# Windowed attention on 32x32 parts of TensorE: four head pairs apart, whole stages in a row, and queries written into their tiles by ScalarE

## The reference

```
q = Wq @ layernorm(x) + bq;  k = Wk @ ctx + bk;  v = Wv @ ctx + bv     # 128 x 1024 each
k, v padded by 8 and 7 columns; window(t) = columns t .. t+15
attn[h,t,:] = softmax(q[h,:,t] . k[h,:,window(t)] * 16**-0.5)
x = x + Wo @ (sum over the window of attn * v) + bo
z = layernorm(x);  w = the two largest gates of softmax(z @ gate_w.T), scaled to sum 1
x = x + sum_e w[:,e] * (z @ lora_A[e].T @ lora_B[e].T)                 # rank 64, 8 experts
```

## Time and profile before

| | |
|---|---|
| median of 3 runs | 1298.94 us |
| the profiled execution | 1300.73 us, its span 1298.8 us, so 1.9 us lie outside the span |
| PE / PEld busy | 94% / 82% of the span |
| DVE, ACT, POOL busy | 69%, 29%, 32% |
| granted TensorE clock, mean | 0.995 of full |
| largest groups on the chain that ended last | L318 (fp32r products), L350 (scores), L363 (weighted sums) |

### The profile page before, as it was taken

How to read it: one execution, slowest core, us unless ns; L and a number is a source line. 1 busy time by engine, 2 the same in 40 slices (tenths; PEclk the granted TensorE clock), 3 DMA queues, 4 the chain that set the end, 5 groups by cost and what they waited for, 6 DMA issues and landing times.

```text
span 1298.8 us, 34642 instructions
## 1 busy us (share of the span) xinstructions
PE 1225.5 (94%) x13953; PEld 1064.8 (82%) x14080; DVE 891.5 (69%) x2021; ACT 380.5 (29%) x553; POOL 416.1 (32%) x300
## 2 busy tenths in 40 slices
PE   3889999999999999999999999999999999999986
PEld 2778888888888888888888888888888888888875
DVE  3777667766767766767766767776767766767653
ACT  3332232322232322232322232322232322232211
POOL 3443333323333332332323333322332322333110
PEclk9989999999999999999999999999999999999999
DMA  6443433343443343443343443243443343443210
GB/s 214 79 88 67 99 91 75 83 90 62 97 91 81 77 97 64 88 93 75 81 95 60 95 92 88 70 99 67 83 93 87 70 99 64 85 93 76 58 40 33
DMA packets 427427, 108.44 MB, mean 83 GB/s; under 512 B 410001, under 2 KB 410129, under 8 KB 427153
## 3 DMA queue, kind: packets, MB, share of 16 engines
q1 hardware_dynamic: 427280, 106.13, 37.6%
HBM read 55.22 MB, written 16.78 MB: 55 GB/s over the span
## 4 chain that ended last, share of the span: by engine, by line
PE 91%; issue 3%; DVE 1%; DMA 1%; POOL 1%; SPq 1%; ACT 0%; POOLq 0%; DVEq 0%
PE bank_a L318 30%; PE bank_b L350 22%; PE bank_b L363 19%; PE bank_c L318 16%; PE bank_a L373 4%; DMA v_diag<-v_t 1%; POOL src_split L873 0%; SPq L237 0%; SPq L246 0%; POOL v_diag L878 0%; DMA ident<-ident_in 0%; DMA raw<-ctx 0%; DVE mid_split L767 0%; DMA q_diag<-q_xn 0%; POOL src_split L883 0%
## 5 line engine op out<-in xcount | busy, mean ns | idle before, releaser
L350 PE MATMUL bank_b<-k_sb,q_diag 64*64 64x32 f32 x8192 | 312.5, 222 | 31.2 <-issue 30.9
L350 PEld LDWEIGHTS bank_b<-k_sb,q_diag 64*64 64x64 f32 x8192 | 271.0, 136 | 83.9 <-issue 71.7
L363 PEld LDWEIGHTS bank_b<-prob_t,v_diag 128*128 128x128 f32 x2304 | 315.7, 192 | 23.8 <-DMA v_diag<-v_t 4.9
L363 PE MATMUL bank_b<-prob_t,v_diag 128*128 128x96 f32 (+2 forms) x2304 | 326.9, 270 | 4.6 <-DMA v_diag<-v_t 4.6
L318 PE MATMUL bank_a<-down_split,mid_split 128*128 128x264 f32 (+1 forms) x1536 | 267.5, 298 | 2.7 <-DVE mid_split L767 2.7
L867 POOL TENSOR_TENSOR prob<-prob,row_inv 128x512 f32<-128x512 f32 x128 | 146.4, 1144 | 323.4 <-DVE row_inv L726 323.4
L318 PE MATMUL bank_c<-src_split,w_split 128*128 128x512 f32 x576 | 221.1, 459 | 18.0 <-POOL src_split L873 14.2
L318 PEld LDWEIGHTS bank_a<-down_split,mid_split 128*128 128x128 f32 x1536 | 214.9, 189 | 15.9 <-ACT mid_split L548 3.0
L318 PE MATMUL bank_a<-up_split,ht_split 128*128 128x512 f32 x768 | 216.3, 405 | 4.0 <-DVE ht_split L808 3.6
L318 PEld LDWEIGHTS bank_a<-up_split,ht_split 128*128 128x128 f32 x768 | 138.2, 189 | 33.8 <-ACT ht_split L585 4.2
L733 DVE STREAM_TRANSPOSE prob_t<-prob 128x768 f32<-128x768 f32 x128 | 124.6, 973 | 30.4 <-POOL prob L867 30.4
(11 more groups left out here) (68 smaller groups left out, 1087.1 us busy)
## 6 DMA issues: line engine op xcount, KB each, us to landing
v_diag<-v_t SPq DMA_DIRECT2D x128, 132.0 KB, 3.8
raw<-x SPq DMA_DIRECT2D x32, 512.0 KB, 5.9
raw<-ctx SPq DMA_DIRECT2D x32, 512.0 KB, 3.4
q_diag<-q_xn SPq DMA_DIRECT2D x512, 32.0 KB, 2.4
resid_pair<-x SPq DMA_DIRECT2D x32, 512.0 KB, 3.4
out<-resid_pair SPq DMA_DIRECT2D x32, 512.0 KB, 2.6
v_diag<-up_w SPq DMA_DIRECT2D x1, 2048.0 KB, 9.3
prob_t<-down_w SPq DMA_DIRECT2D x1, 780.0 KB, 4.8
```

The costliest lines, as they stand in the source:

```text
L350: last = nc.tensor.matmul(bank_b[m % 2][rows, t * KT:(t + 1) * KT], q_diag[rows, m // 2, n, :], k_sb[rows, at:at + KT], start=False, stop= ...
L363: last = nc.tensor.matmul(bank_b[2 + m % 2][:, lo * PW:hi * PW], v_diag[:, n * P:(n + 1) * P], prob_t[:, at:at + (hi - lo) * KT], start=i ...
```

## The change

The attention is cut into 4 pairs of heads instead of 2 halves (scores) and one whole (weighted sums). `scores_chunk` issues for each tile 4 matmuls, on rows and columns 0-31, 32-63, 64-95 and 96-127 of the array, with a 32 x 32 stationary operand. `weighted_chunk` does the same for the weighted sums. Each of the 4 chunks of a stage is issued whole (`attend`: 64 matmuls of scores of `cur`, then 64 of weighted sums of `prev` or `cur`), without projection or expert matmuls in between, and those are issued as whole stages too.

- ScalarE writes `q_diag` straight from PSUM, with two activations of 128 x 1024 whose scale is a per-channel mask times 0.25 (even heads, odd heads), so the zeros of the blocks are written too. `place_q`, `q_placed` and the zeroing of `q_diag` are gone.
- `v_even` is v transposed in blocks by DVE, as before. The tiles with an odd number need v shifted by 16 keys, `v_odd`, which 8 DMAs of 16 rows x 4 KB copy from `v_even`. The zeroing of `v_diag` is gone.
- `prob` and `prob_t` lose their zero columns. `weights_transpose` is 128 x 512 instead of 128 x 768.
- `k_sb`, `attn`, `q_diag` and the v tiles get two buffers each, and the attention's split values get a tile of their own (`attn_split`).
- The order on ACT, DVE and POOL is rearranged to the new stages.

```diff
-            def scores_group(m, s):
-                for t, n in tiles(m, s):
-                    at = (m * CT + t) * QT
-                    for z in range(HALVES):
-                        rows = slice(z * HALF_P, (z + 1) * HALF_P)
+            def scores_chunk(cur, m):
+                keys = k_sb[cur.parity]
+                for t in range(CT):
+                    n = m * CT + t
+                    for g in range(PAIRS):
+                        rows = slice(PW * g, PW * (g + 1))
                         last = nc.tensor.matmul(bank_b[m % 2][rows, t * KT:(t + 1) * KT],
-                                                q_diag[rows, m // 2, n, :],
-                                                k_sb[rows, at:at + KT], start=False,
+                                                q_diag[rows, cur.parity, n, :],
+                                                keys[rows, n * QT:n * QT + KT], start=False,
                                                 stop=t == CT - 1, skip_group_check=True)
-            def weighted_group(m, s):
-                for i in ((0, 1, 2), (3, 4), (5, 6), (7, 8))[s]:
-                    lo, hi = max(2 * i - 1, 0), min(2 * i + 2, CT)
-                    at = m * PC + 2 * i * STRIDE - (2 * i - lo) * KT
-                    n = m * CT // 2 + i
-                    last = nc.tensor.matmul(bank_b[2 + m % 2][:, lo * PW:hi * PW],
-                                            v_diag[:, n * P:(n + 1) * P],
-                                            prob_t[:, at:at + (hi - lo) * KT],
-                                            start=i == 0, stop=i == CT // 2, skip_group_check=True)
+            def weighted_chunk(b, m):
+                for t in range(CT):
+                    n = m * CT + t
+                    values = (v_even, v_odd)[n % 2][b.parity][:, n // 2 * PW:(n // 2 + 1) * PW]
+                    at = n * PW
+                    for g in range(PAIRS):
+                        rows = slice(PW * g, PW * (g + 1))
+                        last = nc.tensor.matmul(bank_b[2 + m % 2][rows, t * PW:(t + 1) * PW],
+                                                values[rows], prob_t[rows, at:at + PW],
+                                                start=t == 0, stop=t == CT - 1, skip_group_check=True)
+                def attend(m, weighted, k):
+                    if weighted:
+                        open_weighted(weighted, k)
+                    if cur:
+                        if m == 0:
+                            pe.wait_ge(q_out, cur.count(2, 2))
+                        open_scores(cur, m)
+                        scores_chunk(cur, m)
+                    if weighted:
+                        weighted_chunk(weighted, k)
...
-                    nc.scalar.activation(q_xn2[:], bank_c[:], ACT.Identity, bias=bq_scaled[:], scale=SCALE).then_inc(q_out, 1)
+                    for h in range(2):
+                        nc.scalar.activation(q_diag[:, ahead.parity, :, h * QT:(h + 1) * QT],
+                                             bank_c[:].rearrange("p (n i) -> p n i", i=QT), ACT.Identity,
+                                             bias=bq_scaled[:, h:h + 1],
+                                             scale=consts[:, 4 + h:5 + h]).then_inc(q_out, 1)
...
+            def place_v(cur):
+                half = PW // 2
+                source, odd = v_even[cur.parity], v_odd[cur.parity]
                 for g in range(PAIRS):
-                    rows = slice(PW * g, PW * (g + 1))
-                    sp.dma_start(blocks[rows, :, PW * g:PW * (g + 1)],
-                                 v_t[rows, :].rearrange("p (n c) -> p n c", c=PW)).then_inc(v_placed, 16)
+                    low = slice(PW * g, PW * g + half)
+                    high = slice(PW * g + half, PW * (g + 1))
+                    sp.dma_start(odd[low, :], source[high, 0:T]).then_inc(v_placed, 16)
+                    sp.dma_start(odd[high, :], source[low, KT:KT + T]).then_inc(v_placed, 16)
```

More of the change, by code:

```diff
@@ L330, in project_pass @@
                                 source, half, True, True)
-            def tiles(m, s):
-                return [(t, m % 2 * CT + t) for t in range(s * CT // GROUPS, (s + 1) * CT // GROUPS)]
             def open_scores(cur, m):
@@ new lines, in step @@
+                attend(2, cur, 0)
+                if prev:
+                    pe.wait_ge(attn_hi, prev.count(1, 1))
+                    pe.wait_ge(attn_lo, prev.count(1, 1))
+                    if ahead:
+                        pe.wait_ge(q_out, ahead.count(2, 2))
+                    elif cur:
+                        pe.wait_ge(v_out, cur.count(1, 1))
+                    for n in range(6):
+                        last = project_pass(n, bank_c, 3, attn_split)
+                        if n % 3 == 2:
+                            last.then_inc(o_done, 1)
@@ new lines, in step @@
+                if old:
+                    for f in range(FK):
+                        down(1, f)
+                attend(3, cur, 1)
+                if old:
+                    pe.wait_ge(h_done, old.count(2, 2))
+                    transposes(bank_a, h_sb, range(EK)).then_inc(ht_done, 1)
+                if ahead:
+                    pe.wait_ge(ctx_hi, ahead.count(1, 1))
+                    pe.wait_ge(ctx_lo, ahead.count(1, 1))
+                    if prev:
+                        pe.wait_ge(x1_done, prev.count(2, 2))
+                    else:
+                        pe.wait_ge(q_out, ahead.count(2, 2))
+                    for n in range(6):
+                        last = project_pass(n, bank_c, 1, src_split)
+                    last.then_inc(k_done, 1)
@@ L503, in _ @@
+                if old:
+                    pe.wait_ge(ht_hi, old.count(1, 1))
+                    pe.wait_ge(ht_lo, old.count(1, 1))
+                    for n in range(2):
+                        for e in range(EK):
+                            up(n, e)
             steps(pe, step)
@@ L828, in step @@
                     layernorm_stats(1, x1, ln2_step, prev)
[L829 to L832 removed]
+                if cur:
+                    weights_sum(cur, 2)
+                if old:
+                    weigh_experts(old, 1)
                 if prev:
```

361 lines of the change are left out of this document (117 added, 244 removed).

## The result

The changed kernel takes 1613.2 us (median of 4 runs, 1599.7 to 1622.9), the kernel before 1298.8 us beside it: a ratio of 1.241, with a 95% interval of 1.231 to 1.252. It is slower by a quarter, where 1160 us was forecast. The profiled execution is one of 1606.4 us.

The account below looks back on a forecast made before the run. PE was taken as the bound (94% busy, step 39.1 us); a new step of 34.8 us, bound by the round from DVE to PE, takes 32 x (39.1 - 34.8) = 138 us off 1300.73: 1160 us, range 1095 to 1290.

Parts of the forecast that it names:

- The array's overlap: Attention matmuls on PE: four 32 x 32 parts work at once, a record's average near 7 ns.
- t: Time in ns per attention matmul on PE, 512 a step; forecast 14.5, a step being 21.3 + 0.512 t us.
- six-record cut: Timeline of six old score records ending at 0.36 us, read as pairs starting some 10 ns apart, one pair in 58 ns.
- PE's base, 21.3 us: PE's step without attention: 22.1 us, less 1.3 for fewer changes between matmul kinds, plus 0.5 for those that stay.
- The round through DVE: PE waits for DVE: 3.3 us ahead of `h_sb`'s transposes, 1.5 us ahead of the last product; step 34.8 us.
- q by ScalarE, the v copies: ACT's second q write, some 1.1 us more, is hidden; v tile lands at 11.9 us, wanted at 11.8, no cost.
- Half the overlap: Rival: only two parts work at once, t near 29, PE step 36.1 us, 1203 us; 0.26 together with late instructions.
- late instructions: Rival: PE's instruction blocks take 1.07 us, singly 1.9 us, t up to 29 ns; 1200 to 1290, shared chance 0.26.
- the number to keep: Break-even for attention on PE: at t = 35 ns the step equals 39.1 us; below it the change gains.
- The sum of 1160: Whole kernel: 32 steps x (39.1 - 34.8) = 138 us off 1300.73, giving 1163, about 1161, forecast 1160 us.
- The slower rival: Each attention record costs a fixed 29 ns, t = 58, PE step 51.0 us, 1680 us in all; chance 0.24.
- The 1550 us: If record starts average no less than 25 ns, 1024 records give 46.9 us a step, about 1550 us.

Follow-up runs that it names:

- e_pace: TensorE alone, without the attention kernel: long runs of small matmuls between runs of 32 large ones; 216.12 us (one run).
- e_whole2: Kernel before with attention in whole stages, `h_sb` transposes ahead of the k projection, output projection and last expert products behind the last weighted sums; 1218.2 us, ratio 0.937.
- after: The changed kernel itself, with attention on four 32 x 32 parts in whole stages; 1613.2 us, ratio 1.241 to the kernel before.
- e_mixed: Changed kernel, same matmuls in another PE order: half stages of 32 attention matmuls alternate with half projections and expert halves; 1474.9 us, ratio 1.136.
- e_pairs: Changed kernel with half the attention matmuls, each covering two neighbouring tiles with one tile's stationary operand; 1201.6 us (one run).

## Why the prediction was wrong, point by point

- **The array's overlap: right.** Forecast 7 ns a record, measured 8.5 to 9.4 at full clock, so t is 17 to 19 instead of 14.5. The estimate of 29 ns for one 32 x 32 part alone is near too, 32 at full clock (e_pace). The reading of the six-record cut held, and 29 ns was no pace of the array for 32 x 32 parts. The rule of the Trainium skill, "TensorE: Matmul & The Clock Gate" (section "Wait — 56ns, not 53.3ns?"), on 25 ns from start to start does not hold between different parts of the array: they start 8.5 ns apart. Nor does the rule of the Trainium skill, "TensorEngine Tiling (Array Packing)" (section "Restrictions and Gotchas"), on a shared PSUM bank show here: all four parts write `bank_b`, at this pace.
- **PE's base, 21.3 us: too high for the order, too low for the clock.** e_whole2 has 35.8 us a step with 44.3% attention on the chain, so 19.9 us for the rest, 2.2 below the 22.1 of before, where I had priced 0.8. Of these 2.2, 1.2 is issue time that the 22.1 contained and e_whole2 has not. That leaves 1.0 for fewer changes of shape, near their price; what I had wrong is that I left the issue time in the base. In after the same work takes 25.0 us, since part of it runs at the lower clock: 24 products of 256 columns take 4.21 us in the step above and 3.04 in e_whole2.
- **The round through DVE: right in place, half the size for `h_sb`.** Forecast waits of 3.3 and 1.5 us. After hardly shows them (4.5 us in all for `ht_split`); that late instructions hide them is argued from the two runs that have fewer or more evenly spread ones. e_mixed shows 2.5 us a step for `h_sb`, e_pairs 1.3 and 1.8 and a step of 36.0. After's own layout was never seen with its instructions in time.
- **q by ScalarE, the v copies: hidden, as forecast.** PE waits 6.1 us in the whole run for the v tile, once.
- **The step that failed: "Half the overlap", late instructions.** I read the earlier trace rows as 1.07 us for a block, one packet's time, and at worst one block in 1.9 us, hence t of at most 29 ns. A packet's time is how long the transfer lasts, not how often one comes. The trace of e_pace shows about 3.73 us from one to the next when PE only waits for them, so t = 58, above the 35 that I had called the number to keep. The sum of 1160 took t = 14.5 from the array and had no term for the supply at all. The row could not tell it: 136 blocks in 1299 us only says that no more were asked for.
- **The second failed step: no price for the clock.** In the step of 47.6 us, gaps are 10.1 us; attention takes 12.5 us where 512 x 14.5 ns are 7.4; the other work 25.0 where it could be 19.9. I had counted on the full clock throughout without saying so. The last two are, as I read it, in good part the granted clock of 0.50 behind a gap (in e_pace 128 records in 1.93 us instead of 1.28).
- **The slower rival** (t = 58, 1680 us) had the right size for another reason. The array has no fixed pace for a record; the supply has one for an instruction. A turn of after's loop takes 97.3 us on the mean, so a step is 48.6 us, an effective t of (48.6 - 21.3) / 0.512 = 53 ns. That this is so near 58 is in part luck, since it holds the lower clock too. The 1550 us by the Trainium skill's rule of 25 ns ("TensorE: Matmul & The Clock Gate", the same section) is near the measured time by luck: the starts that it speaks of lie 8.5 ns apart here.

Open: why a block takes 3.73 us and how many stand ready. 190 records at the start of e_pace's run and about two stages in the kernel would fit one to two blocks of store, but no run measured it directly. Nor is it known whether the jump at a loop turn's end costs some of that store. Whether the attention as a short hardware loop inside the step, whose instructions would be kept, gets the array's 9 ns in the kernel wasn't tried. The lower clock stands behind gaps in the rows above, and where gaps went it rose, but no run held the gaps and kept the clock, so the 314 us between the two kernels are not parted into gaps and clock.

## What to carry to other kernels

When a change multiplies an engine's instructions, count them against the supply, per stage and not per run: here 256 instructions in some 3.7 us, 15 ns each, with little in store. A mean rate below the supply is no proof that it will do. Cutting a matmul into smaller parts pays only while each instruction still brings more than that of array time; else keep the larger tile, or, where it can be built, a loop short enough to be kept. And price a gap on TensorE at more than its length, because the work behind it ran at half clock.

## What the runs showed that I had not expected

- Instructions reach TensorE in blocks of 256, one per 3.45 to 4.01 us when it waits for nothing else, and PE goes on 1.2 to 1.7 us (median 1.38) behind a block's landing.
- A short hardware loop runs with no block loaded at all (832 records, 11.36 us).
- One 32 x 32 part alone fell to a granted clock of 0.50 at 54.3 us with no gap at all in its records (512 in 24.68 us, mean clock 0.58), where four parts at once had 1.00 until their instructions had run out. So a gap is not the only thing ahead of a lower clock.
- A single gap of 3.04 us cost a step 6.45 us, more than half of it behind the gap.
- Whole stages of equal matmuls, with the old tiles, and `h_sb`'s transposes moved ahead, are worth 81 us (1218 us).
